# Two slots instead of three in the rings of split attention weights, with a semaphore of its own for the stores of the output weights

## The chip, the cores and the metric

The kernel runs as one program on one NeuronCore of a Trainium2 chip. The metric is the device time of one execution in microseconds (us); less is better. Engines are TensorE (PE, its weight loads shown as PEld), VectorE (DVE), ScalarE (ACT), GpSimd (POOL) and SyncE (SP), which here only issues DMAs.

## The reference

One decoder layer over x of 16 sequences, 128 tokens, 256 features, in float32:

```
x = x + attention(layernorm(x))       # 16 heads of 128, rotary Q and K, causal softmax, W_O
x = x + long_conv_gate(layernorm(x))  # causal convolution of k with context*value, 8 groups
x = x + moe(layernorm(x))             # 16 experts, top 4, intermediate 176, shared expert 704
```

In attention Q, K and V are `einsum('btc,ncd->btnd', x, W) + b`, and the result is `einsum('bqnd,ndm->bqm', z, W_O) + b_O`. Only the weights of attention, `W_Q`, `W_K`, `W_V` and `W_O`, are touched by the change.

## The kernel before, in words

Float32 products of weights and activations are done as three products of split operands: a tensor is copied to a rounded high part (`_hi`, type float32r, on ACT) and the rest (`_lo`, on DVE, raw minus high), and PE computes high*high, high*low and low*high (lines 550 to 552 for projections, 830 to 834 for the output weights).

Attention is a pipeline of steps. The batch is cut into `GROUPS` = 4 groups of `GB` = 4 sequences; the 16 heads are 8 `PAIRS`. Step (g, p), with running number s = 8g + p, does on PE, in this order: the value projection of pair p-1 (`project_values`), the output product of pair p-3 (L830 to L834), the transposes of the probabilities of head 0 of pair p-2 (`transpose_probs`, L616), the scores of pair p-1 (L852), the transposes of head 1 (L616), the weighing of values (L630), and last the Q and K projections of pair p into four banks (`project`, L550 to L552, 128x512). For steps 1 and 2 of each group and for late steps of group 0, one half of the values comes between the two weighings (`value_order`). In the first two or three steps the parts for which there is no earlier pair are left out. From group 1 on, pieces of the convolution, the router and the scatter of tokens are threaded in between.

The split weights live in rings of `WRING` slots: `w_hi`, `w_lo` (768 KB a slot each) hold Q, K and V weights of one pair, `wo_hi`, `wo_lo` (256 KB a slot each) the output weights of one pair. Pair p is in slot `W_AT[p]` = p % `WRING`.

In group 0 the splitting is done: at the end of step p, ACT runs `split_hi` for the two halves of pair p+1 (L1067) and then `out_hi` (L1077), and DVE runs `split_lo` (L1461) and `out_lo` (L1467) behind its softmax and rotary work of the step. `out_hi(q)` is done in step q-1, but step 1 does q = 0, 1 and 2 together:

```
for q in range(0 if p == 1 else p + 1, p + 2):
    if p:
        out_hi(q)
```

SP stores each split pair to DRAM for the later groups: `keep(p)` (L415, L416, w) and `keep_wo(q)` (L404, L405, wo). SP is one queue in program order. Its round p of group 0 is: two loads of raw weights of pair p into the two `raw` buffers (L429), some loads of constants, `keep(p-1)`, then `keep_wo(p-1)`; round 2 does `keep_wo(0)` and `keep_wo(1)`. Each waits for the split that it stores.

In groups 1 to 3 SP reloads each pair into its slot (L473, L474, and `load_wo`, L409, L410), once the values and the output product of the pair that had the slot are done. Behind some of these loads SP issues fills with zeros (L421, 2120 KB each, 16 in all; L481, three of 2176 KB), and twice the load of `c_t` (L472). PE waits for all four loads of a slot ahead of the Q projection of its pair.

The waits that keep a slot from being overwritten while its store is under way are those on `w_stored`: both kinds of stores count on it, 64 for one pair.

Of the kernel before, what the change touches and what calls it, by code (L numbers as in the profile page):

```python
# [5 lines left out]
F32 = mybir.dt.float32  # L6
# [5 lines left out]
BATCH, SEQ, D = 16, 128, 256  # L12
# [5 lines left out]
CH = D // 128  # L18
PW = 6 * 128
# [2 lines left out]
SCALE = float(DH) ** -0.5  # L22
MASKED = -1e30

WRING = 3
W_AT = [p % WRING for p in range(PAIRS)]
W_USES = [W_AT.count(i) for i in range(WRING)]
W_NTH = [W_AT[:p].count(W_AT[p]) for p in range(PAIRS)]
# [47 lines left out]
def wo_pair(q):  # L76
    return (q - 2) % PAIRS
# [15 lines left out]
def decoder(nc, x_in, wqkv_in, bqk_in, bv_in, wo_in, bo_in, trig_in, mask_in, ident_in,  # L93
# [5 lines left out]
    wo_dram = nc.dram_tensor("wo_dram", (PAIRS, 2, 128, 2, D), F32, kind="Internal").ap()  # L99
    with ExitStack() as ctx:  # L100
        def sb(name, shape, dt=F32, c=ctx):
            return c.enter_context(nc.sbuf_tensor(name, shape, dt))
# [4 lines left out]
        def sem(name):  # L107
            return ctx.enter_context(nc.semaphore(name))
# [24 lines left out]
        at = 3 * EXPERTS + 2  # L133
# [29 lines left out]
        tctx = ExitStack()  # L163
        w_hi = sb("w_hi", [128, WRING, CH, PW], F32R, tctx)
        w_lo = sb("w_lo", [128, WRING, CH, PW], F32R, tctx)
        xt_hi = sb("xt_hi", [128, CH, GT], F32R, tctx)
        xt_lo = sb("xt_lo", [128, CH, GT], F32R, tctx)
        xhat = sb("xhat", [128, GB, D], c=tctx)
# [9 lines left out]
        z_lo = [sb(f"z_lo{h}", [128, GB, SEQ], F32R, tctx) for h in range(2)]  # L178
        wo_hi = sb("wo_hi", [128, WRING, 2, D], F32R, tctx)
        wo_lo = sb("wo_lo", [128, WRING, 2, D], F32R, tctx)  # L180
        bqk = sb("bqk", [128, PAIRS, 4], c=tctx)
        bv = sb("bv", [128, HEADS], c=tctx)
        bo = sb("bo", [128, D], c=tctx)
# [88 lines left out]
        z_lo_done = sem("z_lo_done")  # L272
        raw_loaded = [sem(f"raw_loaded{i}") for i in range(2)]
        w_stored = [sem(f"w_stored{i}") for i in range(WRING)]
        w_loaded = [sem(f"w_loaded{i}") for i in range(WRING)]
        w_hi_done = sem("w_hi_done")
        w_lo_done = sem("w_lo_done")
# [119 lines left out]
        def _(sp):  # L397
            sp.dma_start(x[:, 0:GB, :], x_in[:, 0:GB, :]).then_inc(x_in_sem[0], 16)
            sp.dma_start(ident[:], ident_in).then_inc(ident_loaded, 16)
            def keep_wo(q):  # L400
                at = W_AT[q]
                sp.wait_ge(wo_hi_done, q + 1)
                sp.wait_ge(wo_lo_done, q + 1)
                sp.dma_start(wo_dram[q, 0], wo_hi[:, at].bitcast(F32)).then_inc(w_stored[at], 16)  # L404
                sp.dma_start(wo_dram[q, 1], wo_lo[:, at].bitcast(F32)).then_inc(w_stored[at], 16)  # L405

            def load_wo(q):
                at = W_AT[q]
                sp.dma_start(wo_hi[:, at].bitcast(F32), wo_dram[q, 0]).then_inc(w_loaded[at], 16)  # L409
                sp.dma_start(wo_lo[:, at].bitcast(F32), wo_dram[q, 1]).then_inc(w_loaded[at], 16)  # L410
# [7 lines left out]
            def fill(q, part):  # L418
                es = slice(part * EXPERTS // PARTS, (part + 1) * EXPERTS // PARTS)
                rows = rows_dram[0:EXPERTS * TOKENS, :].rearrange("(e q p r) d -> q p e r d", q=GROUPS, p=128, r=4)[q]  # L420
                sp.dma_start(rows[:, es], zeros[:].unsqueeze(1).to_broadcast([128, EXPERTS // PARTS, 4, XW])).then_inc(zero_filled[q], 16)  # L421

            n = 0
            for p in range(PAIRS):
# [29 lines left out]
                if p == 2:  # L454
                    keep_wo(0)
                if p > 1:
                    keep_wo(p - 1)
                if p == PAIRS - 1:
                    sp.wait_ge(zero_ready, 1)
                    sp.dma_start(rows_dram[EXPERTS * TOKENS:ROWS, :], zeros[:, 0, :]).then_inc(zero_filled[0], 16)  # L460
            keep(PAIRS - 1)
            keep_wo(PAIRS - 1)
            for g in range(1, GROUPS):
                for p in range(PAIRS):
                    at = W_AT[p]
                    if g == 1 and W_NTH[p] == 0:
                        sp.wait_ge(w_stored[at], 64 * W_USES[at])
                    sp.wait_ge(v_ready, 2 * (PAIRS * (g - 1) + W_BEFORE[p] + 1))
                    sp.wait_ge(wo_done, PAIRS * (g - 1) + W_BEFORE[p] - 1)
                    if g > 1 and p == 3:  # L470
                        sp.wait_ge(y_taken, FILTERS * (g - 1))
                        sp.dma_start(c_t[:], ctxt_in[g - 1]).then_inc(ctxt_loaded, 16)  # L472
                    sp.dma_start(w_hi[:, at].bitcast(F32), w_dram[p, 0]).then_inc(w_loaded[at], 16)  # L473
                    sp.dma_start(w_lo[:, at].bitcast(F32), w_dram[p, 1]).then_inc(w_loaded[at], 16)  # L474
                    load_wo(p)
                    for n, at_step in enumerate(FILL_STEPS):
                        if at_step == (g, p):
                            fill(n // PARTS, n % PARTS)
                    if g == 2 and p < SUMS:
                        rows = sums_dram[p].rearrange("(n p) d -> p n d", p=128)  # L480
                        sp.dma_start(rows, zeros[:, 0, 0:D].unsqueeze(1).to_broadcast([128, TOKENS // 128 + 1, D])).then_inc(sums_zero, 16)  # L481
                    if p == 5:
                        sp.wait_ge(skip_taken, 2 * g)
                        sp.dma_start(ctxg[:], ctx_in[:, g * GB:(g + 1) * GB, :]).then_inc(ctx_loaded, 16)
# [575 lines left out]
        def _(act):  # L1060
            def split_hi(n):
                act.wait_ge(raw_loaded[n % 2], 16 * (n // 2 + 1))
                p = n // CH
                if p >= WRING and n % CH == 0:
                    act.wait_ge(w_stored[W_AT[p]], 64 * W_NTH[p])
                    act.wait_ge(v_ready, 2 * (p - WRING) + 2)
                nc.scalar.copy(w_hi[:, W_AT[p], n % CH, :], raw[n % 2][:]).then_inc(w_hi_done, 1)  # L1067

            def out_hi(q):
                if q == 0:  # L1070
                    act.wait_ge(wo_loaded, 16)
                if q >= WRING:
                    act.wait_ge(w_stored[W_AT[q]], 64 * W_NTH[q])
                if q > WRING + 1:
                    act.wait_ge(wo_done, q - WRING - 1)
                r = wo_pair(q)
                nc.scalar.copy(wo_hi[:, W_AT[q]], wo_raw[:, 2 * r:2 * r + 2, :]).then_inc(wo_hi_done, 1)  # L1077
# [53 lines left out]

            root(0, GB)
            split_hi(0)
            split_hi(1)

            def step(g, p, live, first):
# [73 lines left out]
                if first and p < PAIRS - 1:  # L1210
                    split_hi(2 * p + 2)
                    split_hi(2 * p + 3)
# [3 lines that stand above are left out]
# [845 lines left out]
```

## Time and profile before

| | |
|---|---|
| time, median of 3 runs | 956.32 us |
| lowest and highest run | 954.98, 961.11 us |
| span of the profiled execution | 957.6 us |
| instructions | 19531 |
| PE busy | 919.9 us (96%) |
| DVE, ACT, POOL busy | 771.4, 439.1, 505.0 us |
| HBM traffic | 186 GB/s over the span |

The profiled execution is one execution of the same program; of it the span from first to last instruction is recorded, 957.6 us, which lies 1.3 us above the median of the timed runs and inside their spread, so that no other time of its own is added to it. Busy shares are averages over stages with different limits.

### The profile page before, as it was taken

The page shows a single profiled execution, that of the slowest core. Times are in us where ns is not written, and L with a number is a line of the kernel's source. Part 1 is how long each engine was busy: PE and PEld are TensorE (multiplying, and loading weights), DVE is VectorE, ACT ScalarE, POOL GpSimd, SP SyncE. Part 2 cuts the span into 40 slices and gives each one's busy share as a digit, 9 for nine tenths or more (in the row PEclk, how much of TensorE's full clock was granted, in tenths as well). Part 3 has the DMA queues.
Part 4 walks back from the last instruction along what each step waited for, and adds up shares of the span by engine and source line. Part 5 has one row for each costly group of instructions (what it writes and reads, how often), then busy time and mean ns, then how long its engine had stood idle before and what let it go on. Part 6 is the DMA issues. An engine that isn't in the chain of part 4 may idle for free.

```text
span 957.6 us, 19531 instructions
## 1 busy us (share of the span) xinstructions
PE 919.9 (96%) x6337; PEld 825.6 (86%) x6337; DVE 771.4 (81%) x1704; ACT 439.1 (46%) x1227; POOL 505.0 (53%) x380
## 2 busy tenths in 40 slices
PE   6899999999999999999999999989999999999996
PEld 6789898989899888989888898877887799999985
DVE  6978877977887989877798976765778888888857
ACT  3656745454434654333564333472245444444430
POOL 1453424465453435777453677624626377777760
PEclk9999999999999999999999999998999999999998
DMA  7786389899156952303793231325151277787769
GB/s 267 260 339 238 131 305 388 313 393 364 53 181 246 400 191 105 111 24 117 287 373 115 88 112 48 122 65 237 52 216 69 75 126 130 129 132 129 125 109 314
DMA packets 75586, 179.09 MB, mean 187 GB/s; under 512 B 7777, under 2 KB 42465, under 8 KB 74465
## 3 DMA queue, kind: packets, MB, share of 16 engines
q1 hardware_dynamic: 61040, 158.80, 46.0%
q0 software_dynamic: 14448, 19.05, 12.2%
q8 instruction: 55, 0.90, 0.4%
q14 instruction: 43, 0.34, 0.1%
HBM read 98.35 MB, written 79.47 MB: 186 GB/s over the span
## 4 chain that ended last, share of the span: by engine, by line
PE 76%; DVE 8%; issue 6%; DMA 3%; POOL 3%; ACT 2%; SPq 1%; another core or an unknown queue 0%; DVEq 0%; POOLq 0%; ACTq 0%
PE bank L550 11%; PE bank L552 10%; PE bank L551 10%; PE bank L852 6%; PE bank L630 6%; PE bank L954 3%; POOL xs L1350 3%; PE bank L830 3%; PE bank L616 3%; PE bank L832 3%; PE bank L834 3%; PE bank L656 3%; PE bank L658 2%; PE bank L657 2%; DVE turn L1514 2%
## 5 line engine op out<-in xcount | busy, mean ns | idle before, releaser
L1310 POOL TENSOR_TENSOR z_lo<-prob_t,z_hi 128x512 fp32r<-128x512 f32 x64 | 82.5, 1296 | 191.3 <-ACT z_hi L1197 167.6
L1514 DVE SCALAR_TENSOR_TENSOR turn<-bank,bqk,trig 128x1024 f32<-128x1024 f32 x128 | 160.6, 1277 | 23.3 <-PE bank L552 20.8
L1342 POOL TENSOR_TENSOR rot<-turn 128x512 f32<-128x512 f32 x64 | 101.8, 1591 | 107.4 <-DVE turn L1514 91.9
L1403 POOL DMA_INDIRECT sums<-ysb,token_at x79 | 123.3, 1561 | 57.0 <-DMA sums<-ysb,token_at 26.4
L550 PE MATMUL bank<-xt_hi,w_hi 128*128 128x512 f32 x256 | 105.4, 412 | 3.1 <-DVE xt_lo L1478 1.7
L1183 ACT COPY prob_t<-bank 128x512 f32<-128x512 f32 x64 | 37.5, 586 | 150.9 <-PE bank L616 142.7
L1142 ACT ACTIVATE prob<-prob,negmax 128x128 f32<-128x128 f32 x256 | 99.1, 389 | 2.5 <-DVE negmax L1499 2.4
L552 PE MATMUL bank<-xt_hi,w_lo 128*128 128x512 f32 x256 | 100.0, 391 | 0.0
L551 PE MATMUL bank<-xt_lo,w_hi 128*128 128x512 f32 x256 | 99.7, 390 | 0.0
L1350 POOL DMA_INDIRECT xs<-xh,dest x64 | 71.8, 1122 | 41.9 <-issue 38.3
L1153 ACT COPY v<-bank 128x512 f32<-128x512 f32 x64 | 37.6, 588 | 119.7 <-PE bank L552 118.6
L1372 POOL TENSOR_TENSOR kv<-c_t,v_t 128x512 f32<-128x512 f32 x60 | 70.3, 1198 | 21.0 <-ACT v_t L1110 12.3
L1574 DVE TENSOR_TENSOR zc<-bank,c_t 128x512 f32<-128x512 f32 x64 | 44.1, 690 | 43.6 <-PE bank L658 41.8
L550 PE MATMUL bank<-w_hi,xt_hi 128*128 128x256 f32 x256 | 75.3, 294 | 2.9 <-DVE turn L1514 2.8
L1495 DVE SCALAR_TENSOR_TENSOR prob<-bank,mask 128x512 f32<-128x512 f32 x64 | 43.7, 683 | 39.4 <-PE bank L852 37.3
L830 PE MATMUL bank<-wo_hi,z_hi 128*128 128x256 f32 x256 | 73.3, 286 | 1.8 <-issue 1.6
L551 PE MATMUL bank<-w_lo,xt_hi 128*128 128x256 f32 x256 | 73.1, 286 | 0.0
L552 PE MATMUL bank<-w_hi,xt_lo 128*128 128x256 f32 x256 | 73.1, 285 | 0.0
L832 PE MATMUL bank<-wo_lo,z_hi 128*128 128x256 f32 x256 | 72.8, 284 | 0.0
L834 PE MATMUL bank<-wo_hi,z_lo 128*128 128x256 f32 x256 | 72.7, 284 | 0.0
L630 PE MATMUL bank<-prob_t,v 128*128 128x128 f32 x512 | 68.4, 276 | 4.0 <-ACT prob_t L1189 4.0
L1527 DVE TENSOR_TENSOR rot<-turn 128x512 f32<-128x512 f32 x64 | 71.1, 1153 | 0.0
(201 smaller groups left out, 2663.9 us busy)
## 6 DMA issues: line engine op xcount, KB each, us to landing
xs<-zeros SPq DMA_DIRECT2D x16, 2120.0 KB, 15.6
w_hi<-w_dram SPq DMA_DIRECT2D x24, 768.0 KB, 10.0
w_lo<-w_dram SPq DMA_DIRECT2D x24, 768.0 KB, 9.4
xe_all<-xs SPq DMA_DIRECT2D x79, 132.5 KB
wo_hi<-wo_dram SPq DMA_DIRECT2D x26, 256.0 KB, 9.6
wo_lo<-wo_dram SPq DMA_DIRECT2D x26, 256.0 KB, 11.1
sums<-zeros SPq DMA_DIRECT2D x3, 2176.0 KB, 13.0
raw<-in_wqkv SPq DMA_DIRECT2D x16, 384.0 KB, 4.4
```

Source lines behind the costliest of these rows:

```text
L550: nc.tensor.matmul(o, lh, rh, start=(i == 0), stop=False)
L551: nc.tensor.matmul(o, lh, rl, start=False, stop=False)
L552: last = nc.tensor.matmul(o, ll, rh, start=False, stop=(i == n - 1))
L630: last = nc.tensor.matmul(zt_bank[:, b * 128:(b + 1) * 128], v[p % 2][:, b, h * DH:(h + 1) * DH], prob_t[h][:, b, :], start=True, stop=True)
L830: nc.tensor.matmul(o, z_hi[h][:, b, :], wo_hi[:, at, h, :], start=(r == 0 and b % 2 == 0 and h == 0), stop=False, skip_group_check=True)
L832: nc.tensor.matmul(o, z_hi[h][:, b, :], wo_lo[:, at, h, :], start=False, stop=False, skip_group_check=True)
L834: last = nc.tensor.matmul(o, z_lo[h][:, b, :], wo_hi[:, at, h, :], start=False, stop=(r == PAIRS - 1 and h == 1), skip_group_check=True)
L1142: last = nc.scalar.activation(prob[h][:, b, :], prob[h][:, b, :], ACT.Exp, bias=negmax[:, h, b:b + 1], accum_out=total[:, h, b:b + 1])
L1342: nc.gpsimd.tensor_tensor(rot[m][1][:], turn[m][1], turn[m][2], ALU.add).then_inc(rot_pool, 1)
L1350: nc.gpsimd.indirect_dma_start(rows_dram, bass.IndirectOffsetOnAxis(ap=dest[:, at:at + 1], axis=0), xh[:, n // TOPK, :], None).then_inc(sc ...
L1403: nc.gpsimd.indirect_dma_start(sums_dram[s % SUMS], bass.IndirectOffsetOnAxis(ap=token_at[:, s:s + 1], axis=0), ysb[s % YBUFS][:], None, c ...
L1514: last = nc.vector.scalar_tensor_tensor(turn_all[m][:, 2 * i:2 * i + 2, :], qk_bank[2 * m + i][:].unsqueeze(1).to_broadcast([128, 2, GT]), ...
```

## The change

`WRING` goes from 3 to 2. Unused tensors of the size of the third slots are put behind the rings, so that the tensors after them keep their addresses. The stores of the output weights get semaphores of their own, `wo_stored`, and the waits on `w_stored` count 32 for a pair in place of 64. All tables (`W_AT`, `W_USES`, `W_NTH`, `W_BEFORE`) follow from `WRING`: pair p takes the slot of pair p-2 in place of p-3.

```
-WRING = 3
+WRING = 2
+        sb("room", [128, 2 * CH * PW], c=tctx)
+        sb("wo_room", [128, 2 * 2 * D], c=tctx)
+        wo_stored = [sem(f"wo_stored{i}") for i in range(WRING)]
             def keep_wo(q):
...
-                sp.dma_start(wo_dram[q, 0], wo_hi[:, at].bitcast(F32)).then_inc(w_stored[at], 16)
-                sp.dma_start(wo_dram[q, 1], wo_lo[:, at].bitcast(F32)).then_inc(w_stored[at], 16)
+                sp.dma_start(wo_dram[q, 0], wo_hi[:, at].bitcast(F32)).then_inc(wo_stored[at], 16)
+                sp.dma_start(wo_dram[q, 1], wo_lo[:, at].bitcast(F32)).then_inc(wo_stored[at], 16)
...
                     if g == 1 and W_NTH[p] == 0:
-                        sp.wait_ge(w_stored[at], 64 * W_USES[at])
+                        sp.wait_ge(w_stored[at], 32 * W_USES[at])
+                        sp.wait_ge(wo_stored[at], 32 * W_USES[at])
...
                 if p >= WRING and n % CH == 0:
-                    act.wait_ge(w_stored[W_AT[p]], 64 * W_NTH[p])
+                    act.wait_ge(w_stored[W_AT[p]], 32 * W_NTH[p])
                     act.wait_ge(v_ready, 2 * (p - WRING) + 2)
...
                 if q >= WRING:
-                    act.wait_ge(w_stored[W_AT[q]], 64 * W_NTH[q])
+                    act.wait_ge(wo_stored[W_AT[q]], 32 * W_NTH[q])
                 if q > WRING + 1:
                     act.wait_ge(wo_done, q - WRING - 1)
```

## Rows read from the trace of the kernel before

**Rows 1.** The page: busy time by engine, PE's line.

```profile
PE 919.9 (96%) x6337; PEld 825.6 (86%) x6337; DVE 771.4 (81%) x1704; ACT 439.1 (46%) x1227; POOL 505.0 (53%) x380
```

**Rows 2.** The timeline of ACT around step 1's end: start us, us, instruction.

```profile
29.61 1.55 ACT L1067 CAST w_hi<-raw 128x768 fp32r<-128x768 f32 x2
31.07 1.66 ACT L1077 CAST wo_hi<-wo_raw 128x512 fp32r<-128x512 f32 x3
33.21 0.59 ACT L1153 COPY v<-bank 128x512 f32<-128x512 f32 x1 [0.48 <-PE bank L552]
```

**Rows 3.** The timeline of DVE in the same stretch.

```profile
34.88 2.84 DVE L1530 TENSOR_TENSOR prob<-prob,rtotal 128x512 f32<-128x512 f32 x1
37.65 1.82 DVE L1461 TENSOR_TENSOR w_lo<-raw,w_hi 128x768 fp32r<-128x768 f32 x2
39.38 1.88 DVE L1467 TENSOR_TENSOR wo_lo<-wo_raw,wo_hi 128x512 fp32r<-128x512 f32 x3
41.19 0.68 DVE L1495 SCALAR_TENSOR_TENSOR prob<-bank,mask 128x512 f32<-128x512 f32 x1
```

**Rows 4.** SP in the same stretch: its timeline, then its longest wait there.

```profile
12.45 0.42 SPq L416 DMA_DIRECT2D w_dram<-w_lo  x1
40.14 0.32 SPq L404 DMA_DIRECT2D wo_dram<-wo_hi  x1
40.50 0.43 SPq L405 DMA_DIRECT2D wo_dram<-wo_lo  x1
...
SPq L403 <- DVE wo_lo L1467: 11.5, 1, 11.5
```

**Rows 5.** Line L405 alone, 38 to 46 us: its issues and landings.

```profile
L405 SPq DMA_DIRECT2D wo_dram<-wo_lo x2: 433/444/456, 40.5 to 41.5; - x2
...
DMA to landing us min/median/max: 4.1/4.2/4.3
```

**Rows 6.** The timeline of PE, steps 2 and 3: [idle before <-releaser].

```profile
33.95 0.63 PE L616 MATMUL bank<-ident,prob 128*128 128x128 f32 x4 [0.77 <-ACT v L1153]
35.02 2.06 PE L852 MATMUL bank<-rot 64*128 64x128 f32 x32 [0.45 <-DVE rot L1527]
37.78 0.66 PE L616 MATMUL bank<-ident,prob 128*128 128x128 f32 x4 [0.71 <-DVE prob L1530]
47.60 0.39 PE L550 MATMUL bank<-w_hi,xt_hi 128*128 128x256 f32 x1 [0.46 <-DVE turn L1514]
54.17 2.06 PE L852 MATMUL bank<-rot 64*128 64x128 f32 x32 [1.57 <-issue]
```

**Rows 7.** Stretches just after a PE idle time: engines' busy us, granted clock, DMA share, GB/s.

```profile
728.00:729.00 1.00, 1.00 (x3) 0.73 (x3) 1.00 (x4) 0.00 (x0) 0.69 (x2) 0.50 0.15 55
730.00:732.00 2.00, 2.00 (x9) 1.59 (x8) 0.40 (x1) 1.88 (x3) 1.42 (x2) 0.78 0.19 68
```

**Rows 8.** PE's timeline: after the start, and the first matmul after that idle time.

```profile
4.97 6.10 PE L544 MATMUL bank<-ident 128*128 128x128 f32 x28 [4.97 <-DMA ident<-in_ident]
...
727.29 0.65 PE L599 MATMUL bank<-th,gus_hi 128*128 128x512 f32 x1 [1.69 <-DVE tl L1603]
```

**Rows 9.** DMA issues from 11.9 to 13 us: KB, us to landing.

```profile
w_dram<-w_lo SPq DMA_DIRECT2D x1, 768.0 KB, 13.5
```

**Rows 10.** SP's timeline: a reload of group 1; then PE's, the Q projection of pair 2.

```profile
160.58 0.32 SPq L473 DMA_DIRECT2D w_hi<-w_dram  x1
...
177.51 0.47 PE L550 MATMUL bank<-xt_hi,w_hi 128*128 128x512 f32 x1
```

**Rows 11.** DMA share ahead of it; the fullest reload burst: two issues, last one's landing.

```profile
175.00:176.00 1.00, 1.00 (x11) 1.00 (x11) 1.00 (x5) 0.69 (x2) 0.00 (x0) 1.00 0.01 4
...
296.24 6.51 SPq L473 DMA_DIRECT2D w_hi<-w_dram  x1
...
304.24 0.86 SPq L410 DMA_DIRECT2D wo_lo<-wo_dram  x1
...
wo_lo<-wo_dram SPq DMA_DIRECT2D x1, 256.0 KB, 10.5
```

## The prediction

> **What bounds the kernel now.** The page comes first. PE is busy 96% of the span [rows 1], so any time in which PE is made to stand still, and that it doesn't catch up, is added to the total almost one for one. What the change does to resources is nothing: no instruction of PE, DVE, ACT or POOL is added, removed or resized, and the same bytes move. It changes who has to wait for a slot. So the questions are at which places a slot is asked for earlier than it is free, and what was slack there before. I therefore read the timelines of single engines where the rings are filled (the first 60 us) and where they are refilled (from 126 us on), with SP's queue beside them; the reader is to look at the start times and at the idle time in brackets.
>
> **Part 1: the ring of output weights at the end of step 1.** Step 1 is the only step that splits three pairs of output weights in a row. With three slots they all fit: ACT does the three copies in 1.66 us from 31.07 [rows 2]. With two slots `out_hi(2)` is the second user of slot 0 and must wait until both stores of `keep_wo(0)` have landed. When can they? `keep_wo(0)` needs `out_lo(0)` on DVE, and DVE is behind ACT: it finishes a slow normalisation (2.84 us), then two w_lo of the step (1.82 us), and reaches the first wo_lo at 39.38 [rows 3]. SP stands waiting for that wo_lo for 11.5 us and issues the two stores at 40.14 and 40.50 [rows 4]. The second, a store of 256 KB, takes 4.1 to 4.3 us to land [rows 5]. So slot 0 is free at 40.50 + 4.2 = 44.7 us. None of this chain (DVE's rot, normalisation, splits) depends on what ACT does after its second copy, so these times stay as they are. No circle arises either: `keep_wo(0)` doesn't need the third split.
>
> ACT comes to `out_hi(2)` at about 32.3 and leaves it at 44.7 + 0.6 = 45.3 (0.6 us a copy, from 1.66 us for three). Queued behind it on ACT is the copy of the values of step 2, which began at 33.21 [rows 2], and PE's transposes began 0.15 us behind that copy's end, at 33.95, already waiting for it [rows 6]. They now begin at 45.3 + 0.05 + 0.59 + 0.15 = 46.1 us. The delay there is 46.1 - 33.95 = 12.15 us. Also queued: on DVE `out_lo(2)`, ahead of the mask of step 2, for which the scores aren't there until later anyway; on SP `keep_wo(2)`, which it reaches only after the loads of constants, so later than 46 us. These two cost nothing.
>
> What comes back: while PE stands still DVE and POOL clear their backlog. The idle times of PE in step 2 that were due to DVE go: 0.45 ahead of the scores, 0.71 ahead of the second transposes, and 0.46 ahead of the values of step 3 [rows 6], together 1.62. After the scores DVE has four short operations (about 0.7 us each, 2.8 together) while PE has the transposes, two weighings, half of the values and the first Q projection, over 5 us, so PE leads again. The idle 1.57 ahead of the scores of step 3 [rows 6] comes from POOL's rotary addition, which follows the last rotary work of DVE, which follows PE; I let it stand (end of the range: it goes too). Net: 12.15 - 1.62 = 10.5 us, between 8.9 and 10.7.
>
> **Part 2: the clock after the stall.** PE will have been idle from about 33 to 46 us, which no stretch of this trace shows inside the program. The nearest rows: after an idle time of only 1.69 us ahead of 727.29 [rows 8] the granted clock is 0.50, the lower level of 1.2 GHz, and is back at 2.4 GHz during 730 to 732 (0.78 there) [rows 7]; four such dips are in the trace. At the start, after 4.97 us of idle, 28 matmuls of 128x128 take 6.10 us, 0.22 each [rows 8], where four transposes of the same size at 33.95 take 0.63 us [rows 6], 0.16 each with the drain of the last one in it. So the half rate held some 3.4 us in the short case and up to about 5.7 us at the start. Work done at half rate takes twice as long, so it costs half of these times: 1.7 to 2.9 us; I take 2.3. The lower bound is nothing, if the clock isn't cut.
>
> The Trainium skill, "TensorE: Matmul & The Clock Gate", section "What's actually happening", says that the array's default is the throttled clock and that activity releases it; by that rule a pause of this length ends at the lower clock for certain, and the sum is 12.8; without it the sum would be 10.5. The rows above point the same way.
>
> **Part 3: the other slots in group 0.** `split_hi` of pair p+1 now needs the w stores of pair p-1 in place of p-2. The tightest is pair 2, at 29.61 [rows 2], on `keep(0)`: issued at 12.45 [rows 4], it took 13.5 us behind the load of wo_raw [rows 9], so landed at 26.0: 3.6 us to spare. For later pairs the store is issued two steps (over 30 us) ahead. From q = 3 on, `out_hi` has a step or more as well: slot 1 is stored by about 46, and asked for at the end of step 2, about 59 by then. The wait on `v_ready` is passed already, because ACT itself copied those values earlier in the step, and the one on `wo_done` likewise. Counting the stores apart takes the wo stores out of the wait of `split_hi`; nothing in ACT's timeline waits for them now. All this: 0 us, cover 3.6 us at the least.
>
> **Part 4: the reloads in groups 1 to 3.** Pairs 0 and 1 of each group have the same predecessor in both versions (pairs 6 and 7), so these reloads and the two in the tail don't move. From pair 2 on, a reload goes out about a step later, and so do the fills with zeros and the `c_t` loads behind it. The shortest lead is pair 2's, which must wait for the late half of the values of pair 0 in step 1: that point is the 160.58 at which pair 3 is reloaded today; its projection starts at 177.51 [rows 10], which is 16.9 us. A reload of 2 MB plus one fill sent at 160.58 was through by 175, where the DMA engines stand at 0.01 [rows 11], with the fill behind the reload in the queue, so the reload itself by about 170. Cover some 7 us, if nothing is in front. The worst burst of today (two reloads and two fills) took from 296.24 to 304.24 + 10.5 = 314.7, 18.5 us [rows 11]; the change takes that burst apart, as pair 2 no longer follows pair 1 at once. `c_t` would go out at mid step 2 for use in step 3, half a megabyte at the front of the queue: hidden. 0 us, with 0 to 1.6 us per group (18.5 - 16.9) as the bound, 5 us in all.
>
> **Sum.** 10.5 + 2.3 = 12.8 us on the profiled execution's 957.6, and on the median 956.3 + 12.8 = 969.1 us. Later steps are paced by PE and DVE relative to each other, not by the clock on the wall, and there is no later place where PE waits long for a DMA that was sent early, so nothing gives the time back.
>
> **Rivals.** (a) The stall comes, but with the clock not cut, or POOL's 1.57 recovered as well: 8.9 to 10.7 us, 965 to 967. For it: no row shows a pause of this length; against: the four dips of the trace come with pauses of under 2 us or none. Chance 0.22. (b) Not slower: the wait is hidden by DVE's backlog. Scores of step 2 are done at 37.1 and DVE takes them at 41.19, so 4.1 us of ACT's delay cost nothing. It decides if the stores land before about 33.2 + 4.1 = 37.3 us, which would need the first wo_lo 7.4 us earlier than DVE reaches it, or, for a loss under 9.6 us, some 3 us less than I reckon in all. Result 956 to 965. That DVE does get there sooner (POOL's addition of the output bias slows its 2.84 us normalisation) has nothing in the change for it. Chance 0.12. (c) The stall plus late reloads of pair 2 (or pair 3, 19 us of lead): 969 plus 1.6 to 5, so 971 to 974; against it the empty queue at 175. Chance 0.1. (d) Faster, because the reload bursts are spread and disturb less: PE has no wait for w_loaded today that this could take away. Chance 0.01. The forecast, stall with cut clock, 967.5 to 971: 0.55.
>
> **How the numbers follow.** The likeliest case gives 969.1. A range of 8 in 10 takes the forecast, all of (a) and the lower part of (c), and the scatter of the runs (955 to 961 before): 963 to 973. Within 1% of 956.3 (946.8 to 965.9, about what a measurement of this kernel can tell from no change) lie (b) and the low end of (a): 0.19. Slower by over 1%: 0.80. Faster: 0.01.
>
> **What would show it.** In the changed profile: ACT idle for 12 to 13 us ahead of the third wo_hi copy, released by the DMA wo_dram<-wo_lo; PE idle about 12 us ahead of L616 from 33 to 46 us, and half a clock after it; the values of step 3 at about 60 in place of 47.60; the reload of pair 2 at about 173 with PE not waiting. I am wrong if wo_hi's third copy starts before 40 us, if DVE is at its first wo_lo before 37 us, if PE waits at L550 for w_hi<-w_dram in groups 1 to 3, or if PE's idle times later in the attention shrink by more than 2 us.

## The result and the profile after

| | before | after |
|---|---|---|
| median of 4 runs, us | 955.65 | 970.09 |
| lowest and highest run, us | 953.73, 961.11 | 965.78, 971.58 |
| span of the profiled execution, us | 957.6 | 968.5 |

The ratio of the two is 1.0107, with a 95% interval of 1.0068 to 1.0146: slower by some 10 us (955.65 x 0.0107), between 6.5 and 14. This ratio isn't the quotient of the two medians above, which is 1.0151; how it is formed from the four and four runs is not on record. A second set of runs of the same two kernels, below, gives 1.0107 again, with 1.0081 to 1.0134, and there the quotient of the medians (970.70 and 960.54) is 1.0106.

Line numbers behind the changed lines are 2 to 4 higher than before. First ScalarE's timeline, to be laid beside [rows 2]: start, duration, instruction, and in brackets the idle time before it with what ended it.

```profile
28.97 1.55 ACT L1071 CAST w_hi<-raw 128x768 fp32r<-128x768 f32 x2
30.43 1.14 ACT L1081 CAST wo_hi<-wo_raw 128x512 fp32r<-128x512 f32 x2
42.20 0.62 ACT L1081 CAST wo_hi<-wo_raw 128x512 fp32r<-128x512 f32 x1 [10.64 <-DMA wo_dram<-wo_lo]
42.73 0.58 ACT L1157 COPY v<-bank 128x512 f32<-128x512 f32 x1
```

The three copies that ran in one piece are now two and one, 10.64 us apart, and the releaser named is the store of the first low part. The copy of the values stands right behind. Its cause, VectorE and SyncE, beside [rows 3] and [rows 4]; in the last line is the time from issue to landing of the two stores of L408 in this stretch:

```profile
34.24 2.82 DVE L1534 TENSOR_TENSOR prob<-prob,rtotal 128x512 f32<-128x512 f32 x1
36.99 1.81 DVE L1465 TENSOR_TENSOR w_lo<-raw,w_hi 128x768 fp32r<-128x768 f32 x2
38.72 1.28 DVE L1471 TENSOR_TENSOR wo_lo<-wo_raw,wo_hi 128x512 fp32r<-128x512 f32 x2
42.85 0.69 DVE L1471 TENSOR_TENSOR wo_lo<-wo_raw,wo_hi 128x512 fp32r<-128x512 f32 x1 [2.85 <-ACT wo_hi L1081]
47.62 0.69 DVE L1499 SCALAR_TENSOR_TENSOR prob<-bank,mask 128x512 f32<-128x512 f32 x1 [4.08 <-PE bank L856]
...
39.48 0.32 SPq L407 DMA_DIRECT2D wo_dram<-wo_hi  x1
39.84 0.43 SPq L408 DMA_DIRECT2D wo_dram<-wo_lo  x1
...
DMA to landing us min/median/max: 2.3/2.8/3.2
```

VectorE reaches its first wo_lo when it did before (38.72 against 39.38; this execution starts its first projection 0.65 us earlier, at 12.95 in place of 13.60). SyncE issues the first store 0.76 us after VectorE starts its first wo_lo, as before. The store of the low part of pair 0 is the quicker of the two, 2.3 us, and 39.84 + 2.3 = 42.1 is the moment at which ScalarE goes on. TensorE, beside [rows 6]; the first block is the kernel before, the second the changed kernel:

```profile
13.60 0.47 PE L550 MATMUL bank<-xt_hi,w_hi 128*128 128x512 f32 x1 [1.65 <-DVE xt_lo L1478]
...
41.42 0.47 PE L550 MATMUL bank<-xt_hi,w_hi 128*128 128x512 f32 x1
...
59.78 0.47 PE L550 MATMUL bank<-xt_hi,w_hi 128*128 128x512 f32 x1
```

```profile
12.95 0.47 PE L554 MATMUL bank<-xt_hi,w_hi 128*128 128x512 f32 x1 [1.65 <-DVE xt_lo L1482]
...
43.45 1.09 PE L620 MATMUL bank<-ident,prob 128*128 128x128 f32 x4 [10.90 <-ACT v L1157]
...
51.15 0.47 PE L554 MATMUL bank<-xt_hi,w_hi 128*128 128x512 f32 x1
...
67.46 0.47 PE L554 MATMUL bank<-xt_hi,w_hi 128*128 128x512 f32 x1
```

One idle time of 10.90 us ahead of the transposes, and after it none up to 66 us: the other four of [rows 6] are gone. In each block the first line starts the first projection, and the last two start the Q projections of steps 2 and 3. The shifts, with the 0.65 us of the start added, are 10.4 and 8.3 us. The granted clock (third number from the end) through the stall, where 1.00 is 2.4 GHz and 0.50 is 1.2 GHz:

```profile
33.00:36.00 3.00, 0.00 (x0) 0.00 (x0) 3.00 (x2) 0.00 (x0) 2.92 (x2) 1.00 0.96 399
36.00:38.00 2.00, 0.00 (x0) 0.00 (x0) 2.00 (x3) 0.00 (x0) 0.52 (x1) 0.63 0.07 28
42.00:43.50 1.50, 0.05 (x1) 0.08 (x2) 0.65 (x1) 1.10 (x2) 0.00 (x0) 0.50 1.07 311
45.00:46.00 1.00, 1.00 (x14) 1.00 (x12) 0.00 (x0) 0.16 (x1) 0.00 (x0) 0.50 1.18 310
46.00:47.00 1.00, 1.00 (x16) 1.00 (x16) 0.00 (x0) 0.00 (x0) 0.00 (x0) 0.63 0.75 207
47.00:48.00 1.00, 1.00 (x16) 0.88 (x13) 0.38 (x1) 0.00 (x0) 0.00 (x0) 1.00 0.66 248
```

It falls from 2.4 to 1.2 GHz within the idle time and is back shortly before 47 us, so some 3.3 us of work (43.45 to about 46.7) ran at half rate. Last the refill, pair 2 of group 1, beside [rows 10]:

```profile
168.25 0.32 SPq L477 DMA_DIRECT2D w_hi<-w_dram  x1
...
185.18 0.47 PE L554 MATMUL bank<-xt_hi,w_hi 128*128 128x512 f32 x1
```

16.9 us of lead, and no idle time ahead of the projection; TensorE's list of waits has no line for w_dram.

### The profile page after: what moved, and what is told of

It is laid out like the page before. It is cut to its first block, busy times and chain, and to the rows that moved or that the text cites. A ratio compares the mean times of both kernels' runs of the same rounds, so it can differ in the third digit from the quotient of the medians.

```text
span 968.5 us, 19535 instructions
## 1 busy us (share of the span) xinstructions
PE 919.7 (95%) x6337; PEld 825.1 (85%) x6337; DVE 774.7 (80%) x1704; ACT 438.5 (45%) x1227; POOL 501.3 (52%) x380
## 3 DMA queue, kind: packets, MB, share of 16 engines
q0 software_dynamic: 14448, 19.05, 11.9%
## 4 chain that ended last, share of the span: by engine, by line
PE 76%; DVE 7%; issue 5%; POOL 4%; DMA 3%; ACT 2%; SPq 1%; another core or an unknown queue 0%; DVEq 0%; POOLq 0%
PE bank L554 11%; PE bank L556 10%; PE bank L555 10%; PE bank L856 6%; PE bank L634 5%; POOL xs L1354 3%; PE bank L958 3%; PE bank L834 3%; PE bank L620 3%; PE bank L836 3%; PE bank L838 3%; PE bank L660 3%; PE bank L662 2%; PE bank L661 2%; PE bank L926 2%
## 5 line engine op out<-in xcount | busy, mean ns | idle before, releaser
L1346 POOL TENSOR_TENSOR rot<-turn 128x512 f32<-128x512 f32 x64 | 97.1, 1518 | 109.3 <-DVE turn L1518 93.5
L1376 POOL TENSOR_TENSOR kv<-c_t,v_t 128x512 f32<-128x512 f32 x60 | 70.2, 1197 | 20.3 <-ACT v_t L1114 11.5
L1531 DVE TENSOR_TENSOR rot<-turn 128x512 f32<-128x512 f32 x64 | 73.3, 1187 | 0.0
## 6 DMA issues: line engine op xcount, KB each, us to landing
xs<-zeros SPq DMA_DIRECT2D x16, 2120.0 KB, 12.8
sums<-zeros SPq DMA_DIRECT2D x3, 2176.0 KB, 12.8
```

Of the source, the lines that this page charges most:

```text
L1346: nc.gpsimd.tensor_tensor(rot[m][1][:], turn[m][1], turn[m][2], ALU.add).then_inc(rot_pool, 1)
```

## The experiments

Theory S is the prediction's: all of the loss is ScalarE's wait in step 1. The first four kernels are e1 to e4. Each ratio is against the kernel before, run beside it.

**e1: three slots for the output weights only.** The rings are parted; the reloads of Q, K, V weights stay as late as in the changed kernel. The stores and reloads of the output weights count on semaphores borrowed from `ys_loaded`, and the waits on those at the end of the kernel are raised by as much.

```
+WO_RING = 3
+WO_AT = [p % WO_RING for p in range(PAIRS)]
...
-        wo_hi = sb("wo_hi", [128, WRING, 2, D], F32R, tctx)
+        wo_hi = sb("wo_hi", [128, WO_RING, 2, D], F32R, tctx)
...
-                if q >= WRING:
-                    act.wait_ge(wo_stored[W_AT[q]], 32 * W_NTH[q])
+                if q >= WO_RING:
+                    act.wait_ge(wo_stored[WO_AT[q]], 32 * WO_NTH[q])
```

> Two slots for the Q, K, V weights as in the changed kernel, three for the output weights as before. Theory S (all of the loss is ScalarE waiting in step 1 for slot 0 of the output weights): the wait is gone, the third wo_hi copy starts at about 31.5 us, time within 2 us of the kernel before (954 to 958). Rival R (the later reloads of the Q, K, V weights cost it): the reloads are as late as in the changed kernel, so 966 to 971. Rival T (the tail's larger wait for xe_all is a loss of its own): 957 to 960, with a wait of 4 us or more at that line.

Measured: ratio to the kernel before 1.0013 (0.9992 to 1.0035).

```profile
29.76 1.66 ACT L1090 CAST wo_hi<-wo_raw 128x512 fp32r<-128x512 f32 x3
```

The three copies are one piece again, of 1.66 us as in [rows 2]. The third starts at about 30.9, where the expectation had 31.5. The loss is gone though the Q, K, V ring has two slots and its reloads are late: rival R falls. TensorE's wait for xe_all in its profile is 5.0 us and the time is that of the kernel before, so that wait isn't a loss of the change either (T).

**e2: one wait added to the kernel before.**

```
             def out_hi(q):
...
+                if q == 2:
+                    act.wait_ge(w_stored[0], 64)
```

> The kernel before, three slots in both rings, with one wait added: ScalarE waits ahead of the third output weight copy in step 1 until both stores of the first pair's output weights have landed. Theory S: the whole loss comes back with nothing else changed, 965 to 971 us, and a wait of 10 to 12 us there. Rival R: the time stays at 955 to 958, or recovers most of the stall.

Measured: 1.0096 (1.0069 to 1.0124).

```profile
42.51 0.62 ACT L1079 CAST wo_hi<-wo_raw 128x512 fp32r<-128x512 f32 x1 [10.65 <-DMA wo_dram<-wo_lo]
...
PE bank L616 <- ACT v L1155: 10.9, 1, 10.9
```

The same two waits to 0.01 us, and the same loss within the intervals, with three slots in each ring. The Q projections of steps 2 and 3 are 10.7 and 8.7 us late, against 10.4 and 8.3. One wait is enough; with e1, S is shown from both sides.

**e3: two slots, the first output weights split and stored early.**

In the cut below the first `keep_wo(0)` is SyncE's, the next part ScalarE's, and the last VectorE's. The range of the later splits of step 1 starts at 1 in place of 0.

```
                 if p == 2:
+                    keep_wo(0)
...
-                if p == 2:
-                    keep_wo(0)
...
+                if first and p == 1:
+                    out_hi(0)
                 if live(1):
                     exps(0)
...
+                if first and p == 1:
+                    out_lo(0)
                 if live(1):
```

> The changed kernel with two slots in both rings, but the first pair's output weights are split early in step 1 (ScalarE after the values, VectorE ahead of the mask) and stored ahead of the loads of x. Theory S: the store has landed by about 30 us when slot 0 is asked for at 31 us, no wait, 954 to 959 us. Rival R: 966 or more, since the rings have two slots still.

Measured: 0.9992 (0.9971 to 1.0012). The store goes out 15 us earlier:

```profile
24.91 0.42 SPq L408 DMA_DIRECT2D wo_dram<-wo_lo  x1
...
wo_dram<-wo_lo SPq DMA_DIRECT2D x1, 256.0 KB, 5.0
...
29.90 1.14 ACT L1080 CAST wo_hi<-wo_raw 128x512 fp32r<-128x512 f32 x2
```

It lands at 24.91 + 5.0 = 29.9 us, in time for the third wo_hi copy, which is the second of the pair of copies from 29.90 and so starts at about 30.5. There is only half a microsecond to spare. So two slots cost nothing that can be told if the order of the splits fits them.

**e4: TensorE kept busy in the stall**, to see what the half clock costs.

```
+                if first and p == 2:
+                    for _ in range(86):
+                        nc.tensor.matmul(banks[7][:, 0:128], ident[:], ident[:], start=True, stop=True)
```

> The changed kernel with 86 products of the unit matrix with itself on TensorE in the stall (about 9.5 us of extra work in a bank not in use then). The stall of ScalarE stays. If the half clock after the stall costs its share (about 3 to 4.5 us of work at half rate in the changed kernel, so 1.5 to 2.5 us), the time falls by that: 966 to 968.5 in place of 970, with the granted clock at 1.00 up to 50 us. If the half clock costs nothing, because other engines would be waited for anyway, the time stays at 970.

Measured: 1.0177 (1.0153 to 1.0201), slower than the changed kernel. The size was wrong:

```profile
31.84 19.37 PE L805 MATMUL bank<-ident 128*128 128x128 f32 x172
```

86 products of float32 are 172 matmuls in the trace, 19.4 us, and so the filler itself became the bound. It says nothing on what the clock costs. The second set had the right size, and the changed kernel beside it.

**e5: the same with 44 products.**

> The changed kernel with 44 products of the unit matrix in the stall, each of two passes of 0.11 us, 9.7 us in all: they end at about 41.6 us, ahead of the end of the stall at about 43.3. The stall stays, the clock doesn't fall. If the half clock costs its share: steps 2 and later 2 to 3 us earlier than in the changed kernel (delay of the Q projection of pair 2 about 8 us in place of 10.4), time 0.2 to 0.3% under it. If not: the same time as the changed kernel run beside it.

Measured: 1.0063 (1.0034 to 1.0092).

```profile
31.89 9.99 PE L805 MATMUL bank<-ident 128*128 128x128 f32 x88
43.00 0.63 PE L620 MATMUL bank<-ident,prob 128*128 128x128 f32 x4 [1.12 <-ACT v L1160]
...
38.00:42.00 4.00, 3.88 (x35) 3.68 (x33) 1.54 (x3) 0.25 (x1) 0.00 (x0) 1.00 0.56 206
42.00:46.00 4.00, 3.00 (x40) 2.74 (x41) 1.05 (x2) 1.44 (x3) 0.00 (x0) 1.00 1.05 289
```

The filler ends at 41.9, the stall's end still comes from ScalarE, the granted clock stays at 1.00, and the four transposes take 0.63 us in place of 1.09. ScalarE's wait is 10.52 us, against 10.64.

**e6: the changed kernel again.**

> The changed kernel itself, beside the others on one chip. Theory S: 0.9 to 1.1% over the kernel before. Its profile tells which of the small differences far behind the stall (the wait for xe_all near 765 us, the steps that slip by 1 us) come back and which were of one execution.

Measured: 1.0107 (1.0081 to 1.0134). Against it e5 is 0.4% faster, though the two intervals overlap by 0.1%. The traces give the size more sharply. The Q projection of step 2, counted from the first projection of the same execution and compared with before, is 10.3 us late in e6 (50.75 - 41.42, with 0.94 for the start) and 8.9 in e5 (49.17 - 41.42, with 1.15). The half clock is worth 1.4 us there, under the 2 to 3 us that were expected of e5. The changed kernel's own trace says the same: from the transposes to the Q projection of step 2 it takes 7.70 us (51.15 - 43.45), the kernel before 6.31 without its idle times (41.42 - 33.95 - 0.45 - 0.71). The timed difference, about 4 us, is larger, but its uncertainty of some 3 us reaches down near to this. Behind the attention the profiles of equal kernels wander: single steps of groups 2 and 3 slip by 1 to 1.7 us in one execution and not in another, and the wait for xe_all is 3.5 to 5 us in all of these kernels, e0, e1 and e3 included, but for 1.6 in the profile before and 1.5 in e8.

**e0: only the stores counted apart**, three slots in both rings.

```
-                sp.dma_start(wo_dram[q, 0], wo_hi[:, at].bitcast(F32)).then_inc(w_stored[at], 16)
+                sp.dma_start(wo_dram[q, 0], wo_hi[:, at].bitcast(F32)).then_inc(wo_stored[at], 16)
...
-                    act.wait_ge(w_stored[W_AT[p]], 64 * W_NTH[p])
+                    act.wait_ge(w_stored[W_AT[p]], 32 * W_NTH[p])
```

> Three slots in both rings as before, only the stores of the output weights counted on their own. All theories: no wait is added and none that matters is removed, 0.0% against the kernel before, within 0.3%.

Measured: 1.0015 (0.9991 to 1.0038): nothing that can be told. Here too the stores count on semaphores borrowed from `ys_loaded`. The trace shows what one execution more does without any stall: up to step 18 every Q projection is within 0.02 us of the kernel before, at the last one it is 2.4 us behind.

**e9: the changed kernel with a shorter chain in front of the store.** GpSimd's addition of the output bias runs beside VectorE's normalisation in step 1, which takes 2.8 us there. It is moved, for group 0 alone.

```
-                if p == 1 and live(0):
+                if p == (1 if g else 3) and live(0):
...
                     nc.gpsimd.tensor_tensor(xg, xg, bo[:].unsqueeze(1).to_broadcast([128, GB, D]),
                                             ALU.add).then_inc(bo_added, 1)
```

> The changed kernel with the same move. By theory S the chain is VectorE's normalisation and splits, then the store of the first output weights, then ScalarE. A normalisation that is 2.1 us shorter lets the store go 2.1 us sooner: ScalarE's wait falls from 10.6 to about 8.5 us, and the time by about 2 us (0.2%) against the changed kernel, to 0.85% over the kernel before. If the wait were set by something else (the queue of SyncE, the DMA engines), it stays at 10.6 us.

Measured: 1.0076 (1.0049 to 1.0104).

```profile
34.19 0.68 DVE L1534 TENSOR_TENSOR prob<-prob,rtotal 128x512 f32<-128x512 f32 x1
36.52 1.28 DVE L1471 TENSOR_TENSOR wo_lo<-wo_raw,wo_hi 128x512 fp32r<-128x512 f32 x2
...
40.01 0.62 ACT L1081 CAST wo_hi<-wo_raw 128x512 fp32r<-128x512 f32 x1 [8.50 <-DMA wo_dram<-wo_lo]
```

2.14 us less on VectorE (2.82 to 0.68), 2.14 us less wait on ScalarE (10.64 to 8.50), though neither ScalarE nor the ring was touched. That VectorE's queue sets the length of the stall is shown.

TensorE kept only half of it, which the expectation hadn't foreseen:

```profile
41.26 1.09 PE L620 MATMUL bank<-ident,prob 128*128 128x128 f32 x4 [8.77 <-ACT v L1157]
42.28 3.79 PE L856 MATMUL bank<-rot 64*128 64x128 f32 x32
```

The transposes start 2.15 us sooner than in the changed kernel, with the start of each execution allowed for, but the Q projections of steps 2 and 3 only 1.07 and 1.08 us sooner. The granted clock is back at about 46.9 us here (0.56 on average from 46 to 47 us) and at 46.7 in the changed kernel (0.63), so that 5.6 us of work (41.26 to 46.9) run at half rate and not 3.3; the scores take 3.79 us in place of 3.12. The timed 1.0076 can't be told from the changed kernel's 1.0107 by the intervals.

**e7, e8, e10: a version that beats both.** The same move helps without the stall too: e8 is the kernel before with it, e7 and e10 are e3 with it.

> The kernel with the early split and store of the first output weights (two slots, no stall), and GpSimd's addition of the output bias for group 0 moved from step 1 to step 3, where VectorE isn't the bound. VectorE's normalisation beside it took 2.8 us where others take 0.7: theory: 1.5 to 2.5 us off steps 1 and 2, time 0.1 to 0.25% under the kernel before, if nothing behind absorbs it. Rival: the tail, which waits for GpSimd's scatter (xe_all), absorbs it, and the time is that of the kernel before.

> The kernel before with nothing changed but GpSimd's addition of the output bias for group 0, moved from step 1 to step 3. If the gain of the kernel with early split and moved addition (0.37%) comes from this move: 0.2 to 0.4% under the kernel before, VectorE's normalisation 0.7 us in place of 2.8. If it needs the early split too: 0 to 0.15% under.

> The kernel with early split, early store and moved addition once more, beside the kernel before with the moved addition alone: 0.2 to 0.5% under the kernel before, and within 0.15% of the other.

Measured: e7 0.9963 (0.9942 to 0.9985), e8 0.9976 (0.9952 to 0.9999), e10, the same kernel as e7, 0.9974 (0.9949 to 0.9999). All three lie 0.2 to 0.4% under the kernel before, two of them with an interval that ends at 0.9999, and can't be told from each other. e7 was faster than its expectation of 0.1 to 0.25%, e8 and e10 came as expected. So the gain is in the main the move's, and two slots come at no cost that can be told beside it. In the traces the move is worth 0.8 us at the Q projection of step 2 (e8 against the kernel before), which is less than the timed 0.24%, or 2.3 us, but inside its interval.

## Why the prediction was right, point by point

**Bound and place.** That TensorE bounds and a stall is added almost one for one held: the shift of 8.3 us at step 3 stays within 0.02 us from step 3 through step 16 of the trace. The place, the slot, the chain (wo_lo, SyncE, store, third copy, values, transposes) were as forecast, and e2 makes the loss with that wait alone.

**Length of the stall.** Forecast 12.15 us at the transposes, measured 9.50, or 10.15 from the first projection. The term that was off is the landing of the store of pair 0's low part: 4.1 us in the profile before [rows 5], 2.3 here. ScalarE's wait was 10.64 us where 12.4 followed from my times. This is not scatter between executions. The two lines are that store in e1, without the wait, and in e5, with it:

```profile
wo_dram<-wo_lo SPq DMA_DIRECT2D x1, 256.0 KB, 4.8
...
wo_dram<-wo_lo SPq DMA_DIRECT2D x1, 256.0 KB, 2.4
```

In all six traces in which ScalarE waits (the changed kernel, e2, e4, e5, e6, e9) the landing is 2.3 or 2.4 us; in the three without the wait and with the same order up to it (before, e0, e1) it is 4.1, 4.1 and 4.8. The DMA rate while the stores move is about the same: 365 to 393 GB/s in the kernel before, 369 to 385 in the changed one. So the step of the prediction that failed is its sentence that none of this chain depends on what ScalarE does after its second copy: the times of VectorE and SyncE didn't, the landing did. Which work beside the store delays it stays open. A busy TensorE alone isn't enough, since it is busy in e5 too; and e8, without the wait but with the shorter normalisation, has 2.4 as well.

**What comes back.** The 1.62 us of idle times owed to VectorE's backlog came back as said. The 1.57 us ahead of the scores of step 3, which I let stand, came back too in this pair of traces. They stand before the scores where GpSimd's rotary addition takes 5.20 us, which is so in the profiles of before and e0; it takes 1.7 us in all the others. Among those is e1, with no stall and the same order of instructions, so the idle time can be gone without the stall; but it is gone in all six traces with the stall, and there in two of the three without it. Whether the stall takes it away is therefore not settled, nor is what decides between 5.2 and 1.7 us. Against e1's trace in place of the one before, the Q projection of step 3 is 9.9 us late (67.46 - 12.95 against 56.77 - 12.20), and not 8.3.

**Clock.** Forecast 1.7 to 2.9 us, taken as 2.3. The clock was cut, 3.3 us of work at half rate gives 1.65, and e5 puts its effect on the trace at 1.4. In e9 5.6 us at half rate give 2.8, so stalls of 10.9 and 8.8 us came near the two ends of the range, the shorter stall at the dearer end. The upper end had a weak base: the profile has the granted clock at 1.00 from 4 to 12 us of the kernel before, and only the 0.22 us of each matmul there, against 0.11 for the same product in e5, speaks for a half rate. The rule of the Trainium skill, "TensorE: Matmul & The Clock Gate", section "What's actually happening", that activity is what releases the throttle, agrees with this: with the filler the clock stays at 1.00 through the wait. It doesn't account for every dip: in the kernel before the granted clock is 0.50 from 342 to 345 us with TensorE busy throughout.

**Other slots and reloads.** Forecast 0, measured 0: e1 has all the late reloads of the Q, K, V weights and e0 all the separate counts, and neither can be told from the kernel before. The lead of pair 2 was 16.9 us, to the tenth as worked out.

**Sum.** 12.8 us were forecast. With the terms as measured it is 10.15 + 1.4 - 1.62 = 9.9 if the 1.57 us aren't counted, which is what the trace gives against e1, and 8.3 if they are, which is what it gives against the kernel before. The timed runs have 10.2; the lower end of the second set's interval, 1.0081, is 7.8 us, so they exclude neither. The misses, 2.0 of landing, 0.9 of the clock and perhaps 1.6 of the idle time, all went the same way. The profiled pair goes on from 8.3 at step 3 to 10.2 at the last Q projection and 11.5 at the end, counted from the first projection (10.9 over the spans, 968.5 - 957.6). The 3.2 us behind step 3 come from later steps and the wait for xe_all, which wander in kernels without a stall too: e0 is 2.4 us behind at the last Q projection.

That the median, 970.1, lies so near to the forecast 969.1 is luck in good part: the two medians of four runs lie 14.4 us apart, while the ratio, which both sets of runs give alike, stands for 10.2. A forecast that was 2.6 us too large was added to a base, 956.3, that was low: the kernel before has medians of 959.0, 960.5 and 959.4 us in the later sets of 23 to 29 runs.

**Signs and rivals.** None of the signs of being wrong came: the third copy starts at 42.20, VectorE is at its first wo_lo at 38.72, and TensorE doesn't wait for a reload; the later idle times shrank by 2.03 us (0.46 and 1.57), at the limit that was set. The sizes named as signs were all too large: ScalarE's wait 10.64 for 12 to 13, the values of step 3 at 56.90 for about 60, the reload of pair 2 at 168.25 for about 173. Rival (b), a wait hidden by VectorE's backlog, was refused on the right ground; e9 shows its lever, VectorE's work ahead of the first wo_lo, at one us per us of ScalarE's wait, and half of that at TensorE. Rival (a) has the size that came, 8.9 to 10.7, without its condition: the clock was cut, and it was the landing that was shorter.

## What to carry to other kernels

When a ring loses a slot, look first at the burst that fills it fastest, here three pairs split in one step, and not at the steady state, which had 16.9 us of lead and never waited. The price is read from the slowest queue ahead of the event that frees the slot: the freeing store was sent by SyncE but set by VectorE's backlog, and an engine that waits in order holds up everything behind it, here a copy that TensorE needed. The cure is order, not memory: with the first store sent 15 us earlier, two slots ran as fast as three, within 0.3%. And a duration read beside busy engines isn't the duration of the same transfer when the change itself makes those engines wait.

## What the runs showed of the hardware that wasn't expected

The landing of a 256 KB store with the DMA queue empty ahead of it was 2.3 or 2.4 us in six kernels in which ScalarE waited for it, and 4.1 to 4.8 us in three that are the same up to there and don't wait. A stall that was 2.1 us shorter gave TensorE only 1.1 us, because the clock came back at nearly the same time, 46.9 and 46.7 us, and 5.6 us of work in place of 3.3 ran at half rate. Two VectorE and GpSimd operations side by side shared in two ways: VectorE's two rotary subtractions took 1.27 us and GpSimd's addition 5.20 in two profiles, 2.36 and 1.69 in the others; in the two, GpSimd's addition ended 1.1 us behind the run of VectorE operations beside it (54.07 against 52.94 in the kernel before). And a float32 product of 128x128 with itself is two matmuls in the trace, so that 86 of them took 19.4 us; [rows 8] has it already, where the 14 products at the start of the kernel stand as x28.
